# Retiming the ticks and the order inside a tick of a two-layer transformer kernel on one core

## The chip, the cores and the metric

The kernel runs on one core of a Trainium2 chip, as one launch for the whole computation. The metric is the device time of that core in microseconds (us), of which lower is better. The engines are TensorE (PE: matrix products and transposes), VectorE (DVE), ScalarE (ACT), GpSimd (POOL) and SyncE (SP), whose queue issues every DMA. Each runs its own instruction list in order, and they meet through semaphores.

## What is computed

There are 16 sequences of 512 tokens with 128 channels, in float32. Each goes through two layers:

```python
xn = _layernorm(x)
x = x + _L0_attn_ref(xn, ...) + _L0_ffn_ref(xn, ...)   # 16 causal heads of 64 channels, slopes on the distance
xn = _layernorm(x)
x = x + _L1_attn_ref(xn, ...) + _L1_ffn_ref(xn, ...)   # differential attention: 16 heads of 8, rotary
# each FFN: layernorm, 128 -> 512, silu, 512 -> 128, halved, plus its own input xn
# L1_attn: o1 - lam * o2, RMS-normalised per head, then the output product
```

## The kernel before

**Ticks.** Each sequence's first layer takes 32 ticks, and its second layer runs in the ticks of the next sequence or so. Four ticks make a round: in a round one of the eight pairs of heads of the first attention passes each stage, so several pairs are under way. A constant such as `FA_AT` says at which tick of its sequence a step that occurs once is issued; a function `tick` on each engine says in which order that engine issues what falls into a tick, for the four kinds of tick, r = 0 to 3. There is no scheduler: these numbers and this written order are the whole schedule. The branches under `late(g)` serve the last sequence's end.

**First attention.** `project_q`, `project_k`, `project_v` (L1434) make a pair's inputs; `max_scores0` (L1498) makes the scores of query block q in products of 128 to 512 columns (part 0 holds the blocks 0 and 1, then parts 2 and 3). VectorE's `row_max0` (L1195) adds the slopes, takes the maximum and empties the score tile into `pq`. ScalarE's `exp0` (L947), VectorE's `invert_sums` (L1202) and GpSimd's `scale_probs` (L816) turn it into probabilities. `turn_probs` (L1515) transposes them in three groups, 0 to 2, ScalarE's `copy_turned` (L965) empties those tiles, and `pv0` (L1528) is the product with the values.

**Second attention.** It takes 46 steps, spread over 28 ticks, one or two steps in a tick (part 0 and part 1). A step below 32 makes a pair of top tiles (`second_tops`, L1601), of which VectorE's `row_max1` (L1248) takes the row maxima. A step from 14 on makes a pair of key tiles (`second_keys`, L1587), which ScalarE's `exp1` (L987) empties. `second_values` (`pv1`, L1557) is the product with the values, one for every two key steps.

**Banks.** Two accumulator banks, `pj`, serve in turn the projections, `pv0`, the FFNs, the output products and the 128-wide transposes: a use waits until the one before the last has been read. Five banks, `sc`, serve in turn all score, top, key and turned tiles. `PJ_ORDER` and `TILES` list these uses in TensorE's order, and `bank_free` waits for the reader of the tile that had the bank:

```python
before = tile_before(i, kind, m)
...
pe.wait_ge(done, seq.upto(per, n + 1))
```

Since nearly every step makes two tiles, a step's first tile waits for the second tile of the step three before it, and its second tile waits for the first tile of the step two before it.

**Shapes on TensorE.** The tiles of `sc` are made by products and transposes over 64 of the 128 rows of the array (48 or 51 rows in use in the second attention), so that two of them run beside each other. Everything else uses all 128 rows.

**The other steps that the change names.** `ln_stats` and `ln_apply` (L1144 to L1156) are the norms on VectorE, with `ln_scale` on GpSimd between them. `ffn_act` (L913, L915) on ScalarE and `ffn_dve` (L1164) on VectorE are the FFN's activation, `add_from` (L1171) the sums out of a `pj` bank, `residual0` and `residual1` the residual on GpSimd. `rotate` (L1216 to L1228) is the rotary step with its cut into three bfloat16 parts, which `store_parts` sends to DRAM and `stack` brings back as `QS` and `KS`. `head_norm_a` and `head_norm_b` (L1256 to L1279) are the RMS norm of the heads.

## Time and profile before

| | |
|---|---|
| median of 3 runs | 2565.78 us (2561.99 to 2567.45) |
| the profiled execution | 2568.39 us |
| its span, first to last instruction | 2566.6 us |
| mean granted clock of TensorE | 0.984 |
| busy: PE, DVE, ACT, POOL | 94%, 72%, 73%, 55% |

The 32 ticks of a sequence last 153.2 us in the middle of the run. The time is that of TensorE's list and of what makes TensorE wait. In the timeline a merged row gives the time from the first start to the last end of like instructions. A wait ahead of a row is printed in brackets; a wait between two products of one row shows only in its length.

### The profile page before, as it was taken

To read this page: it belongs to the slowest core of one execution; us is meant where nothing else is said; L and a number is where in the kernel's file an instruction comes from. 1 tells how busy PE (TensorE), PEld (TensorE's weight loads), DVE (VectorE), ACT (ScalarE), POOL (GpSimd) and SP (SyncE) were. 2 spreads that over 40 slices of the span, in tenths; PEclk is the share of its full clock that TensorE was granted. 3 is DMA by queue.
4 is the path that set the end of the run, shared out by engine and by line. 5 is a ranking of instruction groups with operands and counts; after the bars stand their busy time and mean duration, and the time that the engine had idled before them with its cause. 6 is when DMAs were issued, how large, how long until landed. Compare 5 with 4: busy or idle time off the path is not lost.

```text
span 2566.6 us, 60925 instructions
## 1 busy us (share of the span) xinstructions
PE 2409.8 (94%) x22400; PEld 1162.3 (45%) x22400; DVE 1852.2 (72%) x5637; ACT 1881.1 (73%) x4707; POOL 1414.1 (55%) x1356
## 2 busy tenths in 40 slices
PE   6999999999999999999999999999999999999876
PEld 3454444444444445444444444445444444444421
DVE  4448677777877777777776877777777776867675
ACT  4866787777778777787778778777777878778445
POOL 5866474655646466474655646565464655646211
PEclk8999999999999999999999999999999999999978
DMA  3002020110202001020200202002020200202020
GB/s 93 6 6 51 6 55 2 39 22 6 55 6 51 6 18 43 6 55 2 48 13 6 55 6 54 3 18 43 6 55 2 55 6 6 55 2 55 2 55 5
DMA packets 59864, 69.11 MB, mean 27 GB/s; under 512 B 11057, under 2 KB 55345, under 8 KB 56369
## 3 DMA queue, kind: packets, MB, share of 16 engines
q1 hardware_dynamic: 59568, 65.21, 11.2%
q8 instruction: 181, 2.97, 0.5%
q14 instruction: 115, 0.93, 0.1%
HBM read 35.04 MB, written 29.36 MB: 25 GB/s over the span
## 4 chain that ended last, share of the span: by engine, by line
PE 76%; DVE 12%; ACT 6%; issue 3%; DMA 1%; POOL 0%; SPq 0%; POOLq 0%; DVEq 0%; ACTq 0%
PE pj L1434 18%; PE pj L1528 12%; PE sc L1498 11%; PE op L1557 8%; PE sc L1515 5%; PE sc L1601 5%; PE sc L1587 5%; PE pj L1454 5%; PE pj L1544 5%; DVE pq L1195 3%; DVE mx L1248 3%; PE pj L1424 2%; ACT pt L987 2%; DVE y L1216 1%; ACT pt L965 1%
## 5 line engine op out<-in xcount | busy, mean ns | idle before, releaser
L816 POOL TENSOR_SCALAR pq<-pq,rsum 128x128 f32<-128x128 f32 (+3 forms) x1024 | 1111.2, 1099 | 939.5 <-DVE rsum L1202 939.3
L1248 DVE TENSOR_REDUCE mx<-sc 128x1 f32<-128x512 f32 x1024 | 653.7, 682 | 200.7 <-PE sc L1601 199.8
L987 ACT ACTIVATE pt<-sc 128x512 f32<-128x512 f32 x1024 | 557.0, 610 | 196.0 <-PE sc L1587 192.8
L1195 DVE CUSTOM_DVE_ANT_0 pq<-sc,relkey 128x128 f32<-128x128 f32 (+3 forms) x1024 | 450.6, 486 | 213.6 <-PE sc L1498 208.8
L947 ACT ACTIVATE pq<-pq,mx 128x128 f32<-128x128 f32 (+3 forms) x1024 | 572.1, 575 | 6.9 <-DVE mx L1195 6.9
L965 ACT ACTIVATE pt<-sc 128x512 f32<-128x512 f32 (+1 forms) x768 | 356.3, 535 | 214.3 <-PE sc L1515 212.7
L1498 PE MATMUL sc<-K,Q 64*128 64x128 f32 (+3 forms) x2048 | 377.8, 466 | 18.2 <-DVE mx L1248 10.4
L1528 PE MATMUL pj<-pt,v 128*64 128x512 f32 (+3 forms) x2048 | 309.3, 444 | 10.1 <-DVE y L1216 5.8
L1434 PE MATMUL pj<-xnT,wqkv 128*64 128x512 f32 x1024 | 273.1, 622 | 12.3 <-ACT xnT L895 5.5
L1515 PEld LDWEIGHTS sc<-ident,pq 64*128 64x128 f32 x5120 | 203.0, 139 | 170.9 <-issue 131.6
L1515 PE MATMUL sc<-ident,pq 64*128 64x64 f32 x5120 | 235.4, 227 | 26.6 <-DVE mx L1195 22.5
L1557 PE MATMUL op<-pt,v 128*32 128x512 f32 x1920 | 255.7, 605 | 3.7 <-ACT pt L987 3.6
L1601 PE MATMUL sc<-KS,QS 48*128 48x512 bf16 x960 | 232.0, 381 | 22.0 <-DVE mx L1195 13.9
L1498 PEld LDWEIGHTS sc<-K,Q 64*128 64x128 f32 x2048 | 147.5, 186 | 228.5 <-issue 187.1
L1528 PEld LDWEIGHTS pj<-pt,v 128*64 128x64 f32 x2048 | 145.9, 138 | 163.8 <-issue 114.6
L947 ACT ACTIVATION_READ_ACCUMULATOR pq<-pq,mx 128x1 f32 x1024 | 218.5, 213 | 0.0
L1587 PE MATMUL sc<-QS,KS 51*128 51x512 bf16 x960 | 188.6, 384 | 2.8 <-ACT pt L987 0.9
L1434 PE MATMUL pj<-wqkv,xnT 128*64 128x128 f32 x2048 | 140.8, 280 | 5.9 <-ACT att L938 5.8
L1587 PEld LDWEIGHTS sc<-QS,KS 51*128 51x128 bf16 x960 | 47.8, 94 | 195.4 <-issue 153.7
L1601 PEld LDWEIGHTS sc<-KS,QS 48*128 48x128 bf16 x960 | 60.3, 94 | 165.3 <-DVE mx L1248 55.1
L1434 PEld LDWEIGHTS pj<-wqkv,xnT 128*64 128x64 f32 x2048 | 110.1, 137 | 50.3 <-issue 37.6
L913 ACT ACTIVATE tanh<-pj,b1h 128x512 f32<-128x512 f32 x128 | 88.2, 689 | 60.0 <-PE pj L1434 58.7
(117 smaller groups left out, 2807.1 us busy)
## 6 DMA issues: line engine op xcount, KB each, us to landing
scr_p<-y SPq DMA_DIRECT2D x160, 128.0 KB, 2.4
QS<-scr_p SPq DMA_DIRECT2D x30, 384.0 KB, 6.1
KS<-scr_p SPq DMA_DIRECT2D x30, 384.0 KB, 8.7
x_in<-in_L_attn_x SPq DMA_DIRECT2D x16, 256.0 KB, 2.8
scr_p<-tanh SPq DMA_DIRECT2D x32, 128.0 KB, 2.4
out_x<-xres SPq DMA_DIRECT2D x15, 256.0 KB, 2.3
QS<-nrow SPq DMA_DIRECT2D x180, 4.0 KB
wqkv<-in_L_attn_w_qkv SPq DMA_DIRECT2D x1, 1536.0 KB, 6.7
```

The lines of the kernel that those rows point to most:

```text
L816: pool.tensor_scalar(rows, rows, rsum[:, p % NROWS, c:c + 1], None, ALU.mult).then_inc(s_scl, 1)
L947: act.activation(rows, rows, ACT.Exp, scale=-1.0, bias=mx0[:, p % NROWS, c:c + 1], accum_out=lsum[:, p % NROWS, c:c + 1]).then_inc(s_exp0, 1)
L965: act.activation(to[:, :, h, :], sc[tile_bank(i, "tr0", m)][:, 0:cols].rearrange("p (n c) -> p n c", c=HALF), ACT.Copy).then_inc(s_ev, 1)
L987: act.activation(pt1[:, GS * (m % 2) + 2 * j + h, :], sc[tile_bank(i, "st1", 2 * n + h)][:, :], ACT.Exp, scale=float(DS) ** -0.25).then_in ...
L1195: dve.tensor_tensor_reduce(out=pq[:, at:at + width], in0=sc[tile_bank(i, "mx0", m)][:, left:left + width], in1=relkey[:, T - width:T], sca ...
L1248: dve.reduce_max(mx1[:, g % 2, at:at + 1], sc[tile_bank(i, "mx1", 2 * t + h)][:, :], AXIS.X).then_inc(s_mxd1, 1)
L1434: last = pe.matmul(t[r, c * k:c * (k + 1)], w(k)[:, r], x(k), start=True, stop=True)
L1498: last = pe.matmul(sc[tile_bank(i, "mx0", m + j)][:, left:left + width], Q0[r, b, P * row:P * (row + 1)], K0[r, b, 0:width], start=True, s ...
L1515: last = pe.transpose(sc[tile_bank(i, "tr0", m + h)][:, HALF * n:HALF * (n + 1)], pq[r, at:at + P], ident[r, r])
L1528: last = pe.matmul(t[DH * j:DH * (j + 1), P * k:T], v0[:, p % NBUF, k, DH * j:DH * (j + 1)], pt[:, base:base + WIDTH[k]], start=k == 0, st ...
L1557: last = pe.matmul(op[32 * j:32 * (j + 1), :], values1[i.last()][:, k, (GS * g + j) // 2, :], pt1[:, GS * (k % 2) + j, :], start=k == 0, s ...
L1601: pe.matmul(sc[tile_bank(i, "mx1", 2 * t + n)][:, :], queries[r, slot, P * q:P * (q + 1)], keys[r, slot, :], start=True, stop=True).then_i ...
```

## The change

It moves steps and removes or adds none. Each constant below is the tick of a step:

```diff
-X_AT = -19
-LN0_AT = (-15, -8, -1)
-XNT0_AT = -5
+X_AT = -20
+LN0_AT = (-15, -9, -2)
+XNT0_AT = -6
...
-LN1_AT = (47, 48, 54)
+LN1_AT = (46, 48, 54)
...
-STORE_AT = (49, 50)
-STACK_AT = (54, 54)
+STORE_AT = (48, 49)
+STACK_AT = (54, 55)
...
-HID0_AT = (2, 5, 7, 10)
-HID1_AT = (57, 59, 60, 61)
-ADDA_AT = 11
-ADDB_AT = 64
-ADDWA_AT = 35
+HID0_AT = (1, 6, 8, 9)
+HID1_AT = (57, 57, 60, 61)
+ADDA_AT = 12
+ADDB_AT = 63
+ADDWA_AT = 36
...
-HEAD3A_AT = 87
-HEAD3B_AT = 89
+HEAD3A_AT = 88
+HEAD3B_AT = 90
...
-PLN0_AT = (-9, -7)
-PLN1_AT = (47, 48)
-RES0_AT = 0
-RES1_AT = 53
-HEAD3P_AT = 87
-STOREOUT_AT = 91
+PLN0_AT = (-13, -8)
+PLN1_AT = (47, 49)
+RES0_AT = 1
+RES1_AT = 50
+HEAD3P_AT = 89
+STOREOUT_AT = 88
```

Inside a tick, TensorE's order is written anew for all four kinds of tick (with the bank lists `pj_order` and `score_order` to match). The third part of the scores, `max_scores0(i, p, 3)`, goes from the end of tick 2 to the head of tick 3. The top tiles go ahead of the key tiles of the same part, except for part 0 of tick 0, and a 128-row product or a group of others mostly stands between them. Here are tick 1, the head of tick 2, and tick 3 (behind its `else`):

```diff
+                elif r == 1:
+                    second_turns(h, k, 0)
+                    second_tops(h, k, 0)
+                    p, i = pair(g, 3)
+                    if i is not None:
+                        pv0(i, p)
+                    second_keys(h, k, 0)
+                    second_tops(h, k, 1)
+                    second_values(h, k, 0)
+                    second_turns(h, k, 1)
+                    second_keys(h, k, 1)
+                    others(g, h, k)
+                    second_values(h, k, 1)
+                    p, i = pair(g, 0)
+                    if i is not None:
+                        max_scores0(i, p, 2)
+                elif r == 2:
+                    second_tops(h, k, 0)
                     second_turns(h, k, 0)
                     p, i = pair(g, -1)
...
+                        project_v(i, p)
+                    second_keys(h, k, 0)
+                    others(g, h, k)
+                    second_tops(h, k, 1)
+                    second_keys(h, k, 1)
                     second_values(h, k, 0)
...
-                    second_turns(h, k, 1)
-                    p, i = pair(g, 0)
-                    if i is not None:
-                        max_scores0(i, p, 3)
                     second_values(h, k, 1)
                 else:
                     second_turns(h, k, 0)
+                    p, i = pair(g, 0)
+                    if i is not None:
+                        max_scores0(i, p, 3)
+                    second_values(h, k, 0)
+                    second_tops(h, k, 0)
+                    others(g, h, k)
                     second_turns(h, k, 1)
                     second_keys(h, k, 0)
-                    second_tops(h, k, 0)
-                    second_values(h, k, 0)
-                    others(g, h, k)
                     p, i = pair(g, 1)
                     if i is not None:
                         turn_probs(i, p, 0)
+                    second_tops(h, k, 1)
                     second_values(h, k, 1)
                     second_keys(h, k, 1)
```

ScalarE and VectorE:

```diff
+                    p, i = pair(g, -1)
+                    if i is not None:
+                        copy_q(i, p)
                     p, i = pair(g, 1)
                     if i is not None:
                         exp0(i, p, 3)
-                    p, i = pair(g, -1)
-                    if i is not None:
-                        copy_q(i, p)
                     p, i = pair(g, 2)
                     if i is not None:
                         copy_turned(i, p, 2)
+                    others(g, h, k)
                     p, i = pair(g, 2)
                     if i is not None:
...
-                    others(g, h, k)
                     p, i = pair(g, 3)
                     if i is not None:
                         copy_attention(i, p)
                     second_attention(h, k, 1)
+                    others(g, h, k)
+                    p, i = pair(g, 0)
+                    if i is not None:
+                        exp0(i, p, 1)
                 elif r == 2:
                     second_attention(h, k, 0)
+                    p, i = pair(g, -1)
+                    if i is not None:
+                        values(i, p)
+                    second_attention(h, k, 1)
                     p, i = pair(g, 0)
                     if i is not None:
-                        exp0(i, p, 1)
-                    second_attention(h, k, 1)
-                    p, i = pair(g, -1)
-                    if i is not None:
-                        values(i, p)
+                        exp0(i, p, 2)
                     others(g, h, k)
                 else:
-                    p, i = pair(g, 0)
-                    if i is not None:
...
-                    p, i = pair(g, 1)
-                    if i is not None:
-                        invert_sums(i, p, 1)
                     others(g, h, k)
-                    p, i = pair(g, 1)
-                    if i is not None:
-                        invert_sums(i, p, 2)
+                    norms(g)
                     second_attention(h, k, 0)
-                    norms(g)
                     p, i = pair(g, -1)
...
+                    if i is not None:
+                        invert_sums(i, p, 3)
                 elif r == 1:
-                    p, i = pair(g, 1)
-                    if i is not None:
-                        invert_sums(i, p, 3)
-                    norms(g)
                     second_attention(h, k, 0)
                     second_attention(h, k, 1)
                     others(g, h, k)
+                    norms(g)
                 elif r == 2:
+                    norms(g)
                     p, i = pair(g, 0)
                     if i is not None:
+                        invert_sums(i, p, 0)
+                    others(g, h, k)
+                    p, i = pair(g, 0)
+                    if i is not None:
                         row_max0(i, p, 2)
-                    norms(g)
-                    others(g, h, k)
                     second_attention(h, k, 0)
...
                     second_attention(h, k, 1)
+                    p, i = pair(g, 0)
+                    if i is not None:
+                        invert_sums(i, p, 2)
 
             pipeline(tick)
```

GpSimd scales parts 0 and 1 of a pair in tick 3 of the pair's own round, part 2 in tick 0 and part 3 in tick 2 of the next; before, part 0 was in tick 2 of its own round, part 1 in tick 0, and parts 2 and 3 in tick 2 of the next. SyncE's list is row for row the same in both kernels, since the stores and loads that got other ticks keep their order among each other.

**Place 1, TensorE, ticks 2 and 3 of a middle round.** In these rows L1498 128x512 is part 3 of the scores, L1587 a pair of key tiles, L1601 a pair of top tiles, L1515 group 0 of the turned tiles, L1434 with `hT` a piece of the FFN, and L1557 the second attention's values. Before, from part 3 on:

```order
L1498 MATMUL sc<-K,Q 128x512 x2
L1557 MATMUL op<-pt,v 32x512 x4
L1587 MATMUL sc<-QS,KS 128x512 x2
L1601 MATMUL sc<-KS,QS 128x512 x2
L1434 MATMUL pj<-hT,w 64x512 x2
L1515 MATMUL sc<-ident,pq 128x64 x16
L1557 MATMUL op<-pt,v 32x512 x4
L1587 MATMUL sc<-QS,KS 128x512 x2
L1601 MATMUL sc<-KS,QS 128x512 x2
```

Now, from part 3 on:

```order
L1498 MATMUL sc<-K,Q 128x512 x2
L1601 MATMUL sc<-KS,QS 128x512 x2
L1434 MATMUL pj<-hT,w 64x512 x2
L1587 MATMUL sc<-QS,KS 128x512 x2
L1515 MATMUL sc<-ident,pq 128x64 x16
L1601 MATMUL sc<-KS,QS 128x512 x2
L1557 MATMUL op<-pt,v 32x512 x4
L1587 MATMUL sc<-QS,KS 128x512 x2
```

The pair of key tiles that stood right behind the scores, ahead of the top tiles, now stands behind the piece of the FFN and right ahead of the turned tiles; the second top pair has moved ahead of the values.

**Place 2, TensorE, the end of tick 1 and tick 2.** L1498 128x384 is part 2 of the scores, L1434 with `wqkv,xnT` 64x128 is `project_v`. Before:

```order
L1557 MATMUL op<-pt,v 32x512 x4
L1498 MATMUL sc<-K,Q 128x384 x2
L1587 MATMUL sc<-QS,KS 128x512 x2
L1601 MATMUL sc<-KS,QS 128x512 x2
L1434 MATMUL pj<-wqkv,xnT 64x128 x8
L1587 MATMUL sc<-QS,KS 128x512 x2
L1601 MATMUL sc<-KS,QS 128x512 x2
L1434 MATMUL pj<-hT,w 64x512 x2
L1498 MATMUL sc<-K,Q 128x512 x2
```

Now:

```order
L1557 MATMUL op<-pt,v 32x512 x4
L1498 MATMUL sc<-K,Q 128x384 x2
L1601 MATMUL sc<-KS,QS 128x512 x2
L1434 MATMUL pj<-wqkv,xnT 64x128 x8
L1587 MATMUL sc<-QS,KS 128x512 x2
L1434 MATMUL pj<-hT,w 64x512 x2
L1601 MATMUL sc<-KS,QS 128x512 x2
L1587 MATMUL sc<-QS,KS 128x512 x2
L1557 MATMUL op<-pt,v 32x512 x4
L1498 MATMUL sc<-K,Q 128x512 x2
L1601 MATMUL sc<-KS,QS 128x512 x2
```

The value projection now stands between the top pair and the key pair that follow part 2, where both pairs stood in one piece behind it, and part 3 is no longer in tick 2.

**Place 3, ScalarE, ticks 2 and 3 of the same round.** L987 is `exp1` on a key pair, L932 the copy of the values, L947 `exp0`, L913 and L915 an FFN piece, L965 `copy_turned`. Before:

```order
L987 ACTIVATE pt<-sc 128x512 x2
L932 ACTIVATE v<-pj 128x512
L913 ACTIVATE tanh<-pj,b1h 128x512
L915 ACTIVATE y<-pj,b 128x512
L947 ACTIVATE pq,lsum<-pq,mx 128x384 x2
L987 ACTIVATE pt<-sc 128x512 x2
L913 ACTIVATE tanh<-pj,b1h 128x512
L915 ACTIVATE y<-pj,b 128x512
L965 ACTIVATE pt<-sc 128x8x64 x2
L987 ACTIVATE pt<-sc 128x512 x2
```

Now:

```order
L987 ACTIVATE pt<-sc 128x512 x2
L932 ACTIVATE v<-pj 128x512
L987 ACTIVATE pt<-sc 128x512 x2
L947 ACTIVATE pq,lsum<-pq,mx 128x384 x2
L913 ACTIVATE tanh<-pj,b1h 128x512
L915 ACTIVATE y<-pj,b 128x512
L987 ACTIVATE pt<-sc 128x512 x2
L913 ACTIVATE tanh<-pj,b1h 128x512
L915 ACTIVATE y<-pj,b 128x512
L965 ACTIVATE pt<-sc 128x8x64 x2
L987 ACTIVATE pt<-sc 128x512 x2
```

`exp0` of part 1 has left tick 2 for tick 1, and that of part 2 has moved from the head of tick 3 to ahead of tick 2's FFN piece. In tick 3 `exp1`, the FFN piece and `copy_turned` keep their order, but the key pair that `exp1` empties now comes later.

## Rows read from the trace of the kernel before

**Rows 1.** The head of the page: span, busy time and share of each engine.

```profile
span 2566.6 us, 60925 instructions
...
PE 2409.8 (94%) x22400; PEld 1162.3 (45%) x22400; DVE 1852.2 (72%) x5637; ACT 1881.1 (73%) x4707; POOL 1414.1 (55%) x1356
```

**Rows 2.** Windows of 32 ticks, first, middle, last: busy us and count, clock.

```profile
80.54:233.77 153.23, 140.51 (x1368) 75.69 (x1365) 86.20 (x328) 111.34 (x302) 109.45 (x106) 0.97 0.11 24
...
999.89:1153.12 153.23, 148.00 (x1406) 71.83 (x1402) 115.05 (x352) 117.12 (x294) 87.70 (x84) 1.00 0.11 26
...
2378.91:2532.14 153.23, 127.11 (x898) 48.00 (x898) 110.88 (x237) 71.90 (x147) 27.70 (x27) 0.86 0.11 24
```

**Rows 3.** TensorE timeline: start, duration, instruction, idle before it and its releaser.

```profile
1017.25 0.73 PE L1601 MATMUL sc<-KS,QS 48*128 48x512 bf16 x2
1018.29 1.09 PE L1434 MATMUL pj<-wqkv,xnT 128*64 128x128 f32 x16 [0.32 <-ACT att L938]
...
1021.36 0.38 PE L1601 MATMUL sc<-KS,QS 48*128 48x512 bf16 x1
1022.10 0.39 PE L1601 MATMUL sc<-KS,QS 48*128 48x512 bf16 x1 [0.36 <-DVE mx L1195]
```

**Rows 4.** The same timeline, later second tiles behind a score tile.

```profile
1039.08 0.38 PE L1601 MATMUL sc<-KS,QS 48*128 48x512 bf16 x1
1039.68 0.39 PE L1601 MATMUL sc<-KS,QS 48*128 48x512 bf16 x1 [0.23 <-DVE mx L1195]
...
1060.09 0.65 PE L1601 MATMUL sc<-KS,QS 48*128 48x512 bf16 x2
...
1064.61 0.39 PE L1601 MATMUL sc<-KS,QS 48*128 48x512 bf16 x1 [0.36 <-DVE mx L1195]
```

**Rows 5.** The same timeline, score products of part 2, and two top pairs.

```profile
1058.81 0.92 PE L1498 MATMUL sc<-K,Q 64*128 64x384 f32 x4 [0.56 <-ACT pt L987]
...
1151.02 0.92 PE L1498 MATMUL sc<-K,Q 64*128 64x384 f32 x4 [0.66 <-DVE mx L1248]
1151.74 0.77 PE L1601 MATMUL sc<-KS,QS 48*128 48x512 bf16 x2
...
1153.47 0.71 PE L1601 MATMUL sc<-KS,QS 48*128 48x512 bf16 x2
```

**Rows 6.** The same timeline, products that wait for a projection bank.

```profile
1008.95 1.08 PE L1434 MATMUL pj<-xnT,wqkv 128*64 128x512 f32 x4 [0.18 <-DVE xres L1171]
...
1116.34 2.37 PE L1528 MATMUL pj<-pt,v 128*64 128x512 f32 x16 [0.49 <-DVE y L1216]
...
1127.02 1.94 PE L1434 MATMUL pj<-xnT,wqkv 128*64 128x512 f32 x8 [0.40 <-ACT xnT L895]
...
1132.77 2.38 PE L1528 MATMUL pj<-pt,v 128*64 128x512 f32 x16 [0.20 <-ACT y L915]
```

**Rows 7.** The same timeline, a pair ahead of a pair, and ahead of a projection.

```profile
1028.88 0.39 PE L1587 MATMUL sc<-QS,KS 51*128 51x512 bf16 x2
1029.10 0.38 PE L1601 MATMUL sc<-KS,QS 48*128 48x512 bf16 x2
1029.41 1.08 PE L1434 MATMUL pj<-xnT,wqkv 128*64 128x512 f32 x4
```

**Rows 8.** Timeline of ScalarE: start, duration, instruction.

```profile
1045.28 1.10 ACT L987 ACTIVATE pt<-sc 128x512 f32<-128x512 f32 x2
1046.29 0.69 ACT L913 ACTIVATE tanh<-pj,b1h 128x512 f32<-128x512 f32 x1
...
1047.44 1.08 ACT L965 ACTIVATE pt<-sc 128x512 f32<-128x512 f32 x2
```

**Rows 9.** TensorE timeline again, the turned tiles of group 0 and the values.

```profile
1046.17 0.71 PE L1515 MATMUL sc<-ident,pq 64*128 64x64 f32 x16
1046.81 1.07 PE L1557 MATMUL op<-pt,v 128*32 128x512 f32 x8
```

**Rows 10.** One line of VectorE: count, ns (least, median, longest), first and last start.

```profile
L1228 DVE TENSOR_TENSOR tanh<-y x28: 691/1172/1659, 345.2 to 2346.7; 128x512 bf16<-128x512 f32 x28
```

72 lines of the change are left out of this document (28 added, 44 removed).

## The prediction

> **What bounds the kernel now.** The head of the page comes first: TensorE is busy for 2409.8 us of a span of 2566.6, with VectorE, ScalarE and GpSimd well below it [rows 1]. So the time is TensorE's list plus what holds it up. The windows say where: the middle sequences all look alike, 153.2 us for 32 ticks, 148.0 of it busy at a granted clock of 1.00, while the first window has 140.5 busy and the last 127.1 [rows 2]. Busy time hides part of the waits, because a pair of half-row products in which the second waits is printed as one longer row. I therefore went through one sequence in TensorE's timeline, from 1001 to 1154 us, and took each start that comes later than the same pair of instructions starts elsewhere. What I looked for in each row is which tile's bank was late, and whose reader was last.
>
> Unheld, the second tile of a top pair starts with the first and the row lasts 0.39 us (the form is seen in [rows 7]). Four kinds of wait stand out.
>
> (a) A top pair close behind part 2 of the scores: its second tile takes the bank that part 2's first tile had two steps before, and VectorE has not emptied it. The row at 1017.25 lasts 0.73 [rows 3], so 0.34 is wait; 0.60 passes between 1039.08 and 1039.68, and the row at 1060.09 lasts 0.65, so 0.26 [rows 4]; the row at 1151.74 lasts 0.77, so 0.38 [rows 5]. Sum 1.58 us.
>
> (b) The same behind part 3: 1021.36 to 1022.10, 0.74 [rows 3]; as much again ahead of 1064.61, which has the same printed idle of 0.36 [rows 4]; and the row at 1153.47, 0.71, so 0.32 [rows 5]. Sum 1.80.
>
> (c) Part 2 itself, behind two step pairs in one piece: 0.56 and 0.66 [rows 5]. Sum 1.22.
>
> (d) A product that needs a `pj` bank: behind the attention copy 0.32 [rows 3], behind a sum 0.18, behind the rotary product 0.49, behind the copy of the transposed norm 0.40, behind an FFN piece 0.20 [rows 6]. Sum 1.59.
>
> Together 6.2 us of a sequence's 153.2. The rest of the list is products back to back.
>
> **The change, part by part.** No step is added or removed, so the terms are waits that go, waits that come, and crossings between shapes.
>
> *Waits (a).* In the new tick 2 only the top pair follows part 2 directly, and its second tile waits for a key or top tile of the step before part 2, long read. The next pair is the key pair, and `project_v` stands in between; a projection's row is 1.08 us long [rows 7], more than any of the four waits. Where there is no key pair (1017 us), the next tile is part 3, also behind `project_v`. I take all 1.58 as gone; at worst the late `row_max0` costs the same again.
>
> *Waits (b).* Part 3 now heads tick 3, and between the top pair behind it and the next tiles stand the others of that tick (an FFN piece, an output product or a transpose in nearly every round). I take the 1.80 as gone.
>
> *Waits (c).* In tick 1 `pv0` now stands between the two step pairs, 2.3 us of a row of 2.37 [rows 6]. The tiles that part 2 waits for are then read. 1.22 gone.
>
> *Waits (d).* ScalarE's attention copy goes ahead of tick 1's FFN piece, `exp0` of part 2 leaves the head of tick 3, where it stood ahead of the transposed norms' copy; `copy_q` goes ahead of `exp0` of part 3; the second FFN's sum and the key rotation's product get ahead of their consumer. I take 1.59 gone, of which 0.2 to 0.5 (the rotary one) hangs on VectorE being free.
>
> *Crossings.* A pair costs 0.22 us from its start to the next when the next is a half-row pair (1028.88 to 1029.10) and 0.31 when it is a projection over all rows (1029.10 to 1029.41) [rows 7], so each crossing from half to all rows costs 0.09. Counted over a middle sequence in both orders there are 64 such crossings before and 61 after: 0.27 less. The Trainium skill, TensorEngine Tiling (Array Packing), Key Properties, says that changing the tiling mode drains TensorE, whichever way it changes. By that rule all changes of array shape would count, 134 before and 129 after, and at the same 0.09 the saving would be 0.45 us. The rows show it in one direction only, and I keep 0.27.
>
> *Waits that come.* In tick 3 the key pair now stands directly ahead of group 0 of the turned tiles, both read by ScalarE, and the last key pair of the tick takes the bank of the first turned tile. In the round with FFN pieces in both ticks 2 and 3, ScalarE has to do `exp1` (1.01 us to the next start), the FFN piece (1.15) and the first of two copies (0.5) before that bank is free [rows 8], 2.7 us, and by then it is still 0.4 behind with tick 2's piece and `exp0` (an estimate from the same rows). TensorE needs 2.2 us from the key pair to there: 0.22 for the pair, 0.64 for the turned tiles, 0.31 for a top pair [rows 7] and 1.0 for the values [rows 9]. The difference is a wait of some 0.9 us, where there is none now; I take 0.85. Four smaller ones of 0.2 to 0.4: in tick 2 behind the output product, where `ln_stats` now stands ahead of `row_max0`; the heads' transpose, whose copy now stands behind `exp0` of part 1; a key projection behind the last heads' norm; and the first top pair behind turned group 2 in the round where the sequence changes. They are estimates by the waits of the same kinds in [rows 5, 6], taken at 0.3: 1.2. The sum of what comes is 2.05, with 0 and 5 as bounds. The wait of 1027 us stays.
>
> *No cost taken.* SyncE's list is unchanged, so no DMA moves past another. GpSimd gets its parts earlier and more evenly; all its results are needed a round later. VectorE's inversions are small and stand later in a tick than their sums. The moved sums, norms and residuals have their readers ticks away; if that cover failed, each would cost about one operation, 0.7 us as in the pieces of [rows 8].
>
> **The sum.** Gone 6.19 + 0.27 = 6.46; come 2.05; net 4.4 us a sequence. In my laying out, about eight places pass within 0.2 us of a bank that is still being read; I take 0.1 each, 0.8 in all, off it. That leaves 3.6 us. Fourteen windows are like the middle one, and the fuller start and the thinner end count as half of one [rows 2], so 14.5 x 3.6 = 52 us. The profiled execution took 2568.4 us, 2.6 more than the median of the runs; 2568.4 - 52 = 2516, and 2.6 less on the scale of the median: 2514.
>
> **The rivals.**
>
> *Gain mostly given back to ScalarE (2548).* Key pair and turned group stand together in five of the eight rounds. If all five wait 0.6 or so rather than one 0.85, 2.4 us more come, 1.2 net remain, 17 us. For it: ScalarE is the fullest engine behind TensorE [rows 1]. Against: before, the same copies waited on nothing.
>
> *VectorE slowed by GpSimd (2537).* The last operation of a rotation takes 0.69 us at least and 1.66 at most, with a median of 1.17 [rows 10]: in the timeline the long ones are those during GpSimd's work on big tiles. GpSimd's scaling has been moved to other ticks. If now both rotations of a sequence are hit instead of one, in three operations each, VectorE loses up to 1.6 us at a place where the projections wait for it: 3.6 becomes 2.0, 29 us gained. The Trainium skill, Advanced Engine Details and Errata, GPSIMD Details, says that GpSimd shares a read and a write interface with VectorE and conflicts with its instructions of two SBUF inputs; the trace agrees for this line.
>
> *Nothing (2566).* The waits only move on to the next bank, because the readers need the same time in total. Against: VectorE and ScalarE are idle for over a quarter of the time [rows 1].
>
> *Slower (2606).* The queue on ScalarE in tick 3 grows into a steady wait: in each of the five rounds TensorE stands for `exp1` and more, 1.6 us on average, 8.0 a sequence against 6.46 less the 1.2: 2.7 us lost, 14.5 times, 40 us. It decides from 1.05 us a round on. For it: `exp1` plus an FFN piece is 2.2 us [rows 8], and `exp0`'s two new places at the ends of ticks 1 and 2 stand ahead of it. Against: in three of the five rounds tick 3 has no FFN piece.
>
> **How the numbers follow.** The forecast, 2490 to 2538 by its own bounds (waits that come between 0.8 and 4), has 0.62. ScalarE taking most back 0.13, VectorE slowed 0.06, nothing 0.06, slower 0.13. A run of this kernel tells 0.2%, some 5 us, from no change. So faster is 0.62 + 0.13 + 0.06 = 0.81, same 0.06, slower 0.13. A range from 2482 (nothing comes, 14.5 x 5.9) to 2564 leaves out the slower case and a little at either end.
>
> **What would show it.** In the profile after, a middle window of 32 ticks lasts about 149.6 us. In TensorE's timeline the top pair behind part 2 lasts 0.4, and the steps of tick 3 start evenly behind part 3; the product of part 2 has no idle ahead of it; the one new wait is a key product's second tile on ScalarE's L965. The forecast is wrong if that wait is found in every round, if L1195 comes up ahead of L1587 in tick 2, or if L1228 is at 1.6 us in both of its instances.

## The result, and the profile after

The changed kernel takes 2530.47 us (median of 4 runs, 2529.27 to 2533.2), the kernel before 2566.61 us (4 runs, 2561.99 to 2569.62) beside it. The ratio is 0.9857, 95% interval 0.9846 to 0.9869: 36 us less. The forecast was 2514, 52 us less. The direction and the range held, and the gain is two thirds of what was forecast. It also comes from other places than forecast.

The head of the page after, span and the busy time of each engine, answers to [rows 1]:

```profile
span 2531.4 us, 60926 instructions
PE 2404.7 (95%) x22400; PEld 1164.7 (46%) x22400; DVE 1850.6 (73%) x5637; ACT 1886.1 (75%) x4707; POOL 1417.6 (56%) x1356
```

TensorE's busy time has fallen by 5.1 us only, the span by 35.2. The windows of 32 ticks after, two of the middle ones (columns: busy time of each engine with its instructions, granted clock, DMA share, GB/s), answer to [rows 2]:

```profile
814.40:966.10 151.70, 147.85 (x1403) 72.02 (x1402) 115.13 (x352) 117.56 (x295) 87.80 (x84) 1.00 0.12 26
966.10:1117.80 151.70, 147.85 (x1404) 72.04 (x1402) 115.11 (x352) 117.57 (x295) 87.82 (x84) 1.00 0.12 26
```

A middle window is 151.7 us long, where 149.6 was forecast and 153.2 is that of before. To see where the 35 us are, I cut both traces at the start of each sequence's first query projection:

| stretch | before | after | difference |
|---|---|---|---|
| first sequence | 95.04 | 83.54 | -11.5 |
| second | 114.08 | 109.97 | -4.1 |
| 13 middle ones, sum | 1992.7 | 1972.6 | -20.1 |
| from the last one on, to TensorE's last product | 347.5 | 348.1 | +0.6 |

So a middle sequence gives 1.5 us and not 3.6, and the start, which the forecast counted as a part of half a window, gives 15.6.

**The start.** Three rows of TensorE's timeline of the kernel before, the last engine named being what was waited for:

```profile
58.48 5.38 PE L1454 MATMUL pj<-w,y 128*64 128x128 f32 x64 [3.34 <-DVE y L1164]
100.01 0.46 PE L1515 MATMUL sc<-ident,pq 64*128 64x64 f32 x8 [2.71 <-DVE mx L1195]
100.41 4.04 PE L1528 MATMUL pj<-pt,v 128*64 128x512 f32 x16
```

The same FFN product in the timeline of the kernel after:

```profile
51.47 1.13 PE L1498 MATMUL sc<-K,Q 64*128 64x512 f32 x4
52.52 3.71 PE L1454 MATMUL pj<-w,y 128*64 128x128 f32 x64
```

Before, TensorE waited 3.34 us for the last `ffn_dve`, which stood at tick 10 of VectorE's list behind the second layer's weights being unpacked, work of the first sequence alone. The product that followed took 5.38 us instead of 3.71. The granted clock from 58.40 to 64.00 us was 0.70; from 52.2 to 56.8 after it was 1.00. Behind the wait of 2.71 us the values product took 4.04 us where its like takes 2.37 [rows 6]. A wait in the start is paid more than once, since the clock falls behind it: granted were 1.00 in the wait itself (55.0 to 58.5 us), then 0.50 from 59.5 to 62.8, and 0.50 again from 100.5 to 103.7 behind the second one. With the 1.67 us that each product took longer, that is 5.0 us at the first place and 4.4 at the second. Another 1.6 us of the difference is no merit of the change: the two projections from 21.7 us took 3.57 us before and 1.94 after, by the clock alone, and that varies between executions (it is 3.68 in e9 below, whose list up to there is that of the kernel after). These three make 11.0 of the 11.5 us. Of the 4.1 us of the second sequence, 1.5 are what each middle one gains. The rest isn't divided here, and part of it can be the clock too: the granted clock in this stretch was 0.97 before, 0.98 after, and 1.00 in e6 and e8 below, where the stretch lasts 108.2 and 106.9 us.

**A middle sequence.** Of each TensorE instruction I took the time from the start of the one ahead of it, and called what exceeds the shortest such time of the same two kinds anywhere in the run a wait. Waits of 0.1 us and more, by who released them, in us of one middle sequence (from 1000.95 us before, from 966.1 after):

| released by | before | after |
|---|---|---|
| `row_max0` | 2.91 | 0.45 |
| `row_max1` | 1.54 | 1.55 |
| attention copy, copies of transposed norms, `rotate` | 1.58 | 0.20 |
| `exp1` | 0.71 | 2.97 |
| turned copies (L965) | 1.35 | 2.06 |
| values copy | 0 | 0.43 |
| FFN piece, sum | 0.53 | 0.57 |
| none near | 0.71 | 0.81 |
| sum | 9.3 | 9.0 |
| the products without their waits | 134.6 | 133.7 |

The waits on `row_max0` and on the copies of the `pj` banks went as the change was made to do it, 3.8 us in all; on `row_max1` as much came as went. Waits on ScalarE's `exp1` and copies of 3.4 us came in their place. The gain of 1.5 us is what this leaves of the waits, 0.3 us, then 0.9 in the products' own list and 0.3 in waits under 0.1 us.

The top pair behind part 2 of the scores, which was to last 0.4 us, does so in one of the four rounds that had a wait there before. These are the four rows of TensorE's timeline after:

```profile
974.66 0.69 PE L1601 MATMUL sc<-KS,QS 48*128 48x512 bf16 x2
...
993.19 0.52 PE L1601 MATMUL sc<-KS,QS 48*128 48x512 bf16 x2
...
1013.97 0.39 PE L1601 MATMUL sc<-KS,QS 48*128 48x512 bf16 x2
...
1034.42 0.59 PE L1601 MATMUL sc<-KS,QS 48*128 48x512 bf16 x2
```

So 0.3, 0.13, 0 and 0.2 us of wait remain there, 0.63 where it was 1.58.

TensorE's timeline of a middle sequence after, at tick 3 of the round that [rows 8] and [rows 9] show and at ticks 1 and 2 near the end of the second attention:

```profile
1020.46 0.39 PE L1587 MATMUL sc<-QS,KS 51*128 51x512 bf16 x2
1021.39 0.71 PE L1515 MATMUL sc<-ident,pq 64*128 64x64 f32 x16 [0.54 <-DVE mx L1248]
1021.91 0.41 PE L1601 MATMUL sc<-KS,QS 48*128 48x512 bf16 x2
1022.25 1.07 PE L1557 MATMUL op<-pt,v 128*32 128x512 f32 x8
1023.25 0.80 PE L1587 MATMUL sc<-QS,KS 51*128 51x512 bf16 x2
...
1075.39 1.07 PE L1557 MATMUL op<-pt,v 128*32 128x512 f32 x8 [0.37 <-ACT pt L987]
...
1079.82 1.06 PE L1557 MATMUL op<-pt,v 128*32 128x512 f32 x8 [0.37 <-ACT pt L987]
```

The last key pair of tick 3 at 1023.25 lasts 0.80 instead of 0.39: its second tile waits 0.41 for the copy of turned group 0, the wait that was forecast (at 0.85). Three lines above, at 1021.39, the first turned tile waits for a row maximum, 0.71 us in all, which was not forecast. And the two values products wait for `exp1`, 0.44 each in all: they start 0.64 us after the last transpose, where the kernel's last sequence has 0.20 (e8's expectation has 0.53 for it; 0.37 is printed idle). No step of the forecast had looked at them. In the groups by line this is TensorE's L1557, whose idle time rose from 3.7 us to this:

```profile
L1557 PE MATMUL op<-pt,v 128*32 128x512 f32 x1920 | 256.7, 607 | 19.7 <-ACT pt L987 18.2
```

**The crossings.** Two value projections of 16 products in TensorE's timeline after, each with the row that follows:

```profile
993.64 1.09 PE L1434 MATMUL pj<-wqkv,xnT 128*64 128x128 f32 x16
994.56 1.03 PE L1434 MATMUL pj<-hT,w 128*64 128x512 f32 x4
...
1014.28 1.09 PE L1434 MATMUL pj<-wqkv,xnT 128*64 128x128 f32 x16
1015.31 0.39 PE L1587 MATMUL sc<-QS,KS 51*128 51x512 bf16 x2
```

From start to start it is 0.92 us when all rows go on and 1.03 when a half-row pair follows. So the crossing costs 0.1 us from all rows to half rows too, beside the 0.09 of the other way [rows 7]. Between 240 and 2200 us of the trace after, the last product of such a projection takes 0.10 us to the start of an FFN or rotary product over all rows (38 times, never more than 0.103) and 0.205 to that of a half-row pair (52 times). There are 64 crossings each way before and 61 after, six fewer, 0.6 us. The Trainium skill, TensorEngine Tiling (Array Packing), Key Properties, says that a change of tiling mode drains TensorE, and names no direction in which it would not; this trace agrees. The prediction had the rule and kept to one direction.

### The profile page after: what moved, and what is told of

Read it like the earlier page. It is cut to its first block, busy times and chain, and to the rows that moved or that the text cites. A ratio compares the mean times of both kernels' runs of the same rounds, so it can differ in the third digit from the quotient of the medians.

```text
span 2531.4 us, 60926 instructions
## 1 busy us (share of the span) xinstructions
PE 2404.7 (95%) x22400; PEld 1164.7 (46%) x22400; DVE 1850.6 (73%) x5637; ACT 1886.1 (75%) x4707; POOL 1417.6 (56%) x1356
## 3 DMA queue, kind: packets, MB, share of 16 engines
q8 instruction: 181, 2.97, 0.5%
## 4 chain that ended last, share of the span: by engine, by line
PE 81%; DVE 9%; ACT 6%; issue 2%; DMA 1%; SPq 0%; POOL 0%; POOLq 0%; ACTq 0%; DVEq 0%
PE pj L1434 20%; PE pj L1528 12%; PE sc L1498 11%; PE op L1557 9%; PE sc L1587 6%; PE sc L1515 5%; PE sc L1601 5%; PE pj L1544 5%; PE pj L1454 5%; ACT pt L987 4%; DVE mx L1248 3%; DVE pq L1195 3%; PE pj L1424 2%; ACT v L932 1%; DVE K L1178 0%
## 5 line engine op out<-in xcount | busy, mean ns | idle before, releaser
L816 POOL TENSOR_SCALAR pq<-pq,rsum 128x128 f32<-128x128 f32 (+3 forms) x1024 | 1126.6, 1113 | 822.6 <-DVE rsum L1202 820.4
L1248 DVE TENSOR_REDUCE mx<-sc 128x1 f32<-128x512 f32 x1024 | 653.2, 681 | 211.0 <-PE sc L1601 211.0
L987 ACT ACTIVATE pt<-sc 128x512 f32<-128x512 f32 x1024 | 556.3, 606 | 337.0 <-PE sc L1587 334.2
L947 ACT ACTIVATE pq<-pq,mx 128x128 f32<-128x128 f32 (+3 forms) x1024 | 574.4, 579 | 15.6 <-DVE mx L1195 15.5
L965 ACT ACTIVATE pt<-sc 128x512 f32<-128x512 f32 (+1 forms) x768 | 357.5, 543 | 77.6 <-PE sc L1515 75.7
L1498 PE MATMUL sc<-K,Q 64*128 64x128 f32 (+3 forms) x2048 | 374.5, 463 | 2.2 <-ACT pt L965 0.3
L1434 PE MATMUL pj<-xnT,wqkv 128*64 128x512 f32 x1024 | 271.6, 618 | 6.8 <-DVE xres L1171 2.9
L1557 PE MATMUL op<-pt,v 128*32 128x512 f32 x1920 | 256.7, 607 | 19.7 <-ACT pt L987 18.2
L1515 PEld LDWEIGHTS sc<-ident,pq 64*128 64x128 f32 x5120 | 208.1, 139 | 145.4 <-issue 121.6
L1515 PE MATMUL sc<-ident,pq 64*128 64x64 f32 x5120 | 232.7, 226 | 30.6 <-DVE mx L1195 20.9
L1498 PEld LDWEIGHTS sc<-K,Q 64*128 64x128 f32 x2048 | 149.3, 186 | 219.1 <-issue 156.9
L1601 PE MATMUL sc<-KS,QS 48*128 48x512 bf16 x960 | 219.6, 386 | 5.3 <-DVE mx L1248 2.3
L947 ACT ACTIVATION_READ_ACCUMULATOR pq<-pq,mx 128x1 f32 x1024 | 222.4, 217 | 0.0
L1587 PE MATMUL sc<-QS,KS 51*128 51x512 bf16 x960 | 204.8, 387 | 5.7 <-ACT pt L987 0.5
L1587 PEld LDWEIGHTS sc<-QS,KS 51*128 51x128 bf16 x960 | 50.8, 93 | 215.3 <-issue 162.2
L1434 PE MATMUL pj<-wqkv,xnT 128*64 128x128 f32 x2048 | 141.8, 281 | 0.0
L1434 PEld LDWEIGHTS pj<-wqkv,xnT 128*64 128x64 f32 x2048 | 110.7, 138 | 50.0 <-issue 47.5
L1601 PEld LDWEIGHTS sc<-KS,QS 48*128 48x128 bf16 x960 | 61.2, 95 | 139.0 <-DVE mx L1248 51.7
L913 ACT ACTIVATE tanh<-pj,b1h 128x512 f32<-128x512 f32 x128 | 87.7, 685 | 48.8 <-PE pj L1434 48.8
```

The costliest lines, as they stand in the source:

```text
L816: pool.tensor_scalar(rows, rows, rsum[:, p % NROWS, c:c + 1], None, ALU.mult).then_inc(s_scl, 1)
L947: act.activation(rows, rows, ACT.Exp, scale=-1.0, bias=mx0[:, p % NROWS, c:c + 1], accum_out=lsum[:, p % NROWS, c:c + 1]).then_inc(s_exp0, 1)
L987: act.activation(pt1[:, GS * (m % 2) + 2 * j + h, :], sc[tile_bank(i, "st1", 2 * n + h)][:, :], ACT.Exp, scale=float(DS) ** -0.25).then_in ...
L1248: dve.reduce_max(mx1[:, g % 2, at:at + 1], sc[tile_bank(i, "mx1", 2 * t + h)][:, :], AXIS.X).then_inc(s_mxd1, 1)
L1434: last = pe.matmul(t[r, c * k:c * (k + 1)], w(k)[:, r], x(k), start=True, stop=True)
L1498: last = pe.matmul(sc[tile_bank(i, "mx0", m + j)][:, left:left + width], Q0[r, b, P * row:P * (row + 1)], K0[r, b, 0:width], start=True, s ...
```

## The experiments

First, second and middle sequence are the stretches of the table above, each from the one execution that was profiled; the middle one is the median of 13. The ratio is to the kernel before timed beside the run. Its median lay between 2565.5 and 2571.2 us from one set of runs to the next, so ratios compare more closely than times. The kernel after has 0.9857 (0.9846 to 0.9869).

| run | us | ratio to before (95%) | first | second | middle |
|---|---|---|---|---|---|
| e1_hid0_only | 2574.3 | 1.0014 (1.0004 to 1.0023) | 91.0 | 115.1 | 153.8 |
| e2_hid0_norm0 | 2582.9 | 1.0048 (1.0035 to 1.0061) | 86.3 | 116.0 | 154.7 |
| e3_ticks_only | 2573.1 | 1.0013 (1.0004 to 1.0021) | 86.7 | 114.0 | 154.2 |
| e4_orders_only | 2603.4 | 1.0124 (1.0111 to 1.0137) | 89.3 | 112.3 | 156.1 |
| e5_orders_norm0 | 2572.6 | 1.0016 (1.0003 to 1.0028) | 89.3 | 110.0 | 154.0 |
| e6_residual_late | 2553.1 | 0.9940 (0.9925 to 0.9954) | 83.5 | 108.2 | 153.3 |
| e7_hidden_later | 2534.4 | 0.9869 (0.9854 to 0.9883) | 83.3 | 109.9 | 151.9 |
| e8_values_late | 2527.1 | 0.9843 (0.9826 to 0.9859) | 83.4 | 106.9 | 151.5 |
| e9_v_behind_keys | 2530.8 | 0.9858 (0.9841 to 0.9874) | 86.9 | 110.0 | 151.7 |
| e10_pv_ahead | 2545.9 | 0.9918 (0.9903 to 0.9933) | 83.6 | 110.1 | 152.9 |
| e11_keys_first | 2537.7 | 0.9887 (0.9872 to 0.9901) | 83.7 | 110.5 | 152.1 |
| e12_copies_half | 2523.9 | 0.9829 (0.9806 to 0.9853) | 85.4 | 110.5 | 151.1 |

**e1 and e2: the start's ticks alone.** The kernel before with `HID0_AT = (1, 6, 8, 9)`, and in e2 the first norm's ticks too:

```diff
-HID0_AT = (2, 5, 7, 10)
+HID0_AT = (1, 6, 8, 9)
-LN0_AT = (-15, -8, -1)
+LN0_AT = (-15, -9, -2)
-PLN0_AT = (-9, -7)
+PLN0_AT = (-13, -8)
```

(e1 has the first pair of lines only; e2 also `X_AT` and `XNT0_AT`, one tick earlier.)

> The kernel before, with HID0_AT = (1, 6, 8, 9) alone. Theory 1: in the first sequence VectorE's last FFN piece stood behind the preparation of the second layer's weights, which made TensorE wait 3.34 us, and the clock that fell in this wait made the output product 5.38 us long instead of 3.71. Then the stretch from the first q projection of sequence 0 to that of sequence 1 (95.0 us) gets shorter by about 5.0 us, and the 32 ticks of a middle sequence stay within 0.5 us of 153.2: 2566 - 5 = 2561. Rival: the shorter start comes from the order inside the ticks; then this changes nothing.

> The kernel before, with HID0_AT and the first norm's four constants (X_AT, LN0_AT, XNT0_AT, PLN0_AT) of the changed one. Theory 1: the wait of 2.71 us ahead of the turned tiles at 100 us, behind the norms of the next sequence on VectorE, and the 1.67 us by which the following values product was longer, go as well: the first 95.0 us shrink by about 9.4, the time to 2557, plus or minus what a middle sequence gives (within 0.5 us each, so 7). Rival: the norms' wait stays, since in the order of before VectorE does them ahead of the scores in that tick anyway; then 2561 as with the FFN pieces alone.

The first sequence falls by 4.0 us and then by 4.7, in all 8.7 where 9.4 was expected. e1 loses the wait of 3.34 us and e2 both waits. The 64 FFN products take 3.71 us in both runs, the values product 2.38 in e2, and 3.55 in e1, which keeps the wait of 2.71 ahead of it. So both terms of the start are what the theory has. The times missed: 2561 and 2557 were expected, and both runs are slower than the kernel before, since the middle sequence rises by 0.6 and 1.5 us and not by under 0.5. The same ticks cost in the old orders.

**e3 and e4: the two halves of the change.** e3 has all the new ticks with the orders of before, e4 all the new orders with the ticks of before.

> All the constants of the changed kernel, the written orders of before. Theory 1 (the middle sequences gain by the order inside the ticks, the start by the constants): a middle sequence stays within 0.5 us of 153.2, the start is 10 to 15 us shorter, time 2551 to 2558. Rival (constants and orders each bring part of both): a middle sequence at about 152.4 and the time at about 2548.

> The written orders of the changed kernel, all constants of before. Theory 1: a middle sequence at 151.7 to 152.3, the start little shorter, time 2541 to 2551. Rival (the orders suit only their own constants): a middle sequence at 153 or more and a time not under 2566.

Neither half makes the kernel faster. For e3 neither the theory nor its rival holds, for e4 the rival does. A middle sequence costs 1.0 us more with the ticks alone and 2.9 more with the orders alone, and 1.5 less with both: 5.4 us a sequence come from the two together. TensorE's timeline of e4 has two waits that neither kernel has in this size:

```profile
811.55 1.08 PE L1434 MATMUL pj<-xnT,w_l 128*64 128x512 f32 x4 [1.22 <-DVE K L1178]
857.67 0.66 PE L1424 MATMUL pj<-ident,hn 128*128 128x128 f32 x4 [2.18 <-DVE hn L1156]
```

**e5: the orders with the first norm's ticks**, the four constants of e2 without `HID0_AT`.

> The written orders of the changed kernel with the first norm's four constants of it (X_AT, LN0_AT, XNT0_AT, PLN0_AT), all other constants of before. Theory 2: the constants have to fit the orders. In the orders alone the transpose of the next sequence's second norm waits 2.25 us for VectorE (L1156), since the new order puts the norm of tick -1 where nothing covers it, and about 1 us more of the products right behind it; with the norm a tick earlier this goes: a middle sequence falls from 156.1 to about 153, the time from 2603 to about 2558. Rival (the loss of the orders alone is spread over many places): not more than 1 us a sequence comes back, 2585 or more.

The wait for `hn` is gone (a middle sequence 154.0 instead of 156.1, where 153 was expected), the wait for the last `copy_k` stays in the same size. On VectorE `ln_apply` heads its tick in both orders. But the new orders have TensorE make the top pair ahead of it behind the 64 products of the FFN: in e4 VectorE takes that pair's maxima from 854.36 us and begins the norm at 855.56, for 2.05 us where it took 1.10 in the kernel before, and TensorE has nothing left to do from 855.5 on. One tick earlier the norm is out of the way; the new orders are affordable only with their ticks.

**e6: the residual back at its tick.** The kernel after with one constant changed:

```diff
-RES1_AT = 50
+RES1_AT = 53
```

> The changed kernel with RES1_AT back at 53. Theory 2: GpSimd's residual over two big tiles then runs beside VectorE's rotation, L1228 or L1224 takes 1.65 us instead of 0.69 in one of the two rotations, the copy of the keys behind it comes late and the second rotary product waits for its bank: 1.0 to 1.4 us more a sequence, 15 to 21 us in all, about 2547. Rival (VectorE has time to spare there): the rotation is 1 us longer and a sequence stays at 151.7.

A middle sequence costs 1.64 us more, as the theory has it (1.0 to 1.4 expected), and the second rotary product waits 1.23 us for `copy_k`, as in e4 and e5. If the two add, the norm's ticks (2.1 us) and this one (1.64) make 3.7 of the 4.4 us that lie between e4's middle sequence and that of the kernel after. VectorE's timeline of e6 ahead of it, then GpSimd's:

```profile
940.75 0.69 DVE L1224 TENSOR_TENSOR y<-y 128x512 f32<-128x512 f32 x1
941.48 1.39 DVE L1226 CAST y<-y 128x512 bf16<-128x512 f32 x1
942.90 1.65 DVE L1228 TENSOR_TENSOR tanh<-y 128x512 bf16<-128x512 f32 x1
944.48 0.68 DVE L1178 COPY K<-pj 128x512 f32<-128x512 f32 x1
```

```profile
941.07 1.51 POOL L801 TENSOR_TENSOR xacc<-xacc,xn 128x512 f32<-128x512 f32 x1
942.66 1.34 POOL L805 TENSOR_TENSOR xacc<-xacc,bias 128x512 f32<-128x512 f32 x1
```

The rotation's last two operations take 1.39 and 1.65 us while GpSimd adds the residual, and `copy_k` behind them is late by that. Each of the two ends only after GpSimd's addition beside it has ended (942.58 and 944.00 us), by 0.29 and 0.55 us. In the kernel after the residual is three ticks earlier, and the rotation's last operation takes 691 ns at least, 693 in the middle and 694 at most, where [rows 10] has 691, 1172 and 1659:

```profile
L1228 DVE TENSOR_TENSOR tanh<-y x32: 691/693/694, 178.4 to 2425.3; 128x512 bf16<-128x512 f32 x32
```

The Trainium skill, Advanced Engine Details and Errata, GPSIMD Details, tells of this conflict; here it is worth 14 times 1.64, 23 us, more than the middle sequences gain. The prediction had the mechanism as a rival in the wrong direction: it feared that the change would add such meetings, and the change takes them away. The kernel before had the meeting too (its operation at 1111.26 us took 1.65), but in its orders a values product stands ahead of the second rotary product, and no wait of 0.1 us or more names `copy_k` in its middle sequence: what waited behind the rotation there was 0.49 [rows 6]. The 1.64 us is what the meeting costs in the new orders.

**e7 and e8: two of the waits that remain.** In e7 VectorE has `row_max0` of part 2 ahead of the others in tick 2; in e8 TensorE has the values product of part 1 in tick 1 behind part 2 of the scores:

```diff
-                    second_values(h, k, 1)
                     p, i = pair(g, 0)
                     if i is not None:
                         max_scores0(i, p, 2)
+                    second_values(h, k, 1)
```

> The changed kernel with VectorE's row_max0 of part 2 ahead of the others in tick 2, instead of behind them. If the wait of 0.71 us ahead of the turned tiles in the round of the second FFN piece comes from that piece standing ahead of row_max0 (0.6 us) on VectorE, it falls to about 0.1, and a sequence to about 151.2; the time falls by up to 8 us, to about 2525. Rival (the wait is for VectorE's three row maxima in sequence, however they start): no change in that wait, 2530 to 2535, since the FFN pieces come later.

> The changed kernel with the values product of part 1 behind part 2 of the scores in tick 1. Theory: the wait of 0.53 us ahead of the values in tick 1 (for exp1 of the key pair just issued) goes, since the scores' 0.9 us stand in between; a sequence falls to about 151.2 and the time by some 7 us. Rival: the score product's bank is not free yet there, and the wait goes over to it: 151.7 as before, 2530.

e7 leaves the 0.71 us at the first turned tile as it was and costs 0.15 us a middle sequence: what is late there isn't the order of tick 2. e8 takes the wait at tick 1 away and gains only 0.2 us a middle sequence, since the transpose in tick 2 now waits for ScalarE's copy into `oraw` (0.23 printed). Its second sequence is 3.1 us shorter, but at a granted clock of 1.00 instead of 0.98, so that is not shown to be its merit. At 2527.1 it is 3.4 us below the kernel after, where the two intervals overlap.

**e9: the value projection behind the key pair.** This undoes in tick 2 what the prediction had the waits (a) go by:

```diff
+                    second_keys(h, k, 0)
                     p, i = pair(g, -1)
                     if i is not None:
                         project_v(i, p)
-                    second_keys(h, k, 0)
```

> The changed kernel, with the value projection of tick 2 of a round behind the key pair, as before the change, and not between the top pair and the key pair. My theory (the prediction's waits (a) were removed by the projection that stands behind the top pair): the key pair's second tile takes a bank that was read late, so waits of 0.3 to 0.6 us come back at that pair in each of the four rounds that have this tick's part 2 or 3 ahead, 1.5 to 2 us a sequence, a middle sequence of 153.3 us and a ratio to the changed kernel of about 1.010, so 2552 us. Rival (the waits of tick 2 went with the smoother supply of score parts, not with the projection's place): no wait comes back, within 4 us of 2530.

The middle sequence is 151.7 us, as after, and the time is 2530.8: my theory falls. One wait came, at one of the four places. TensorE's timeline of e9, the second tile of the key pair:

```profile
866.17 0.38 PE L1587 MATMUL sc<-QS,KS 51*128 51x512 bf16 x1
866.78 0.39 PE L1587 MATMUL sc<-QS,KS 51*128 51x512 bf16 x1 [0.23 <-DVE mx L1195]
```

It is 0.60 us. In exchange three waits behind it are shorter: ahead of part 3 in tick 3 of the next round (0.20 became 0.11), at a values product behind part 3 (0.27 became under 0.10) and at another (0.44 became 0.29). So at three of the four places (a) went with something else in the new lists. Which of it, the place of the top pair or VectorE's order, no run here separates.

**e10: `pv0` ahead of the pairs**, which undoes what the waits (c) were to go by:

```diff
+                    p, i = pair(g, 3)
+                    if i is not None:
+                        pv0(i, p)
                     second_tops(h, k, 0)
-                    p, i = pair(g, 3)
-                    if i is not None:
-                        pv0(i, p)
```

> The changed kernel, with the first layer's values product (pv0) of tick 1 ahead of the top pair, as before the change, so that two top and key pairs follow each other without it. My theory (the prediction's waits (c) were removed by pv0 between the pairs): waits of 0.5 to 0.6 us come back in tick 1 wherever there is a pv0, two or more to a sequence, so 1 to 1.5 us a sequence, a middle sequence of 152.9 and about 2548 us. Rival (banks are free by then in either order): no wait comes back, within 4 us of 2530.

The middle sequence costs 1.18 us more, where (c) was 1.22. Part 2 of the scores waits 0.66 us for `row_max1` again, as in the second row of (c) in [rows 5]. In place of the first, which was for `exp1`, a top pair's second tile waits for `row_max1`; TensorE's timeline of e10:

```profile
886.28 0.38 PE L1601 MATMUL sc<-KS,QS 48*128 48x512 bf16 x1
887.00 0.39 PE L1601 MATMUL sc<-KS,QS 48*128 48x512 bf16 x1 [0.35 <-DVE mx L1248]
```

**e11: the key pair of tick 3 earlier**, ahead of the FFN piece, output product or transpose:

```diff
                     second_tops(h, k, 0)
+                    second_keys(h, k, 0)
                     others(g, h, k)
                     second_turns(h, k, 1)
-                    second_keys(h, k, 0)
```

> The changed kernel, with the key pair of part 0 in tick 3 ahead of the tick's other products (FFN piece, output product or transpose) and not behind them and turned group 1. My theory (the waits of tick 3, 0.4 to 0.5 us in each of five rounds, stand behind ScalarE, which gets exp1 and two turned copies in one piece): exp1 can begin earlier, the waits of the last key pair behind the turned copy fall by half, 1 us a sequence less, a middle sequence of 150.7 and about 2516 us. Rival (ScalarE's whole list of the tick is what is late, so an earlier begin only moves the wait to the pair itself, which takes a bank of part 3's time): the waits stay in sum, 2530 plus or minus 6, or slower.

The rival is right: 0.44 us more a middle sequence. TensorE's timeline of e11:

```profile
848.45 0.37 PE L1587 MATMUL sc<-QS,KS 51*128 51x512 bf16 x1
849.03 0.39 PE L1587 MATMUL sc<-QS,KS 51*128 51x512 bf16 x1 [0.21 <-DVE mx L1195]
849.34 3.71 PE L1544 MATMUL pj<-wout,att 128*64 128x128 f32 x64
...
853.76 0.38 PE L1587 MATMUL sc<-QS,KS 51*128 51x512 bf16 x1
854.48 0.39 PE L1587 MATMUL sc<-QS,KS 51*128 51x512 bf16 x1 [0.35 <-ACT pt L965]
```

The pair now waits for `row_max0` of part 3 (0.58 at the second tile, and 0.73 in two other rounds), and the tile behind the turned copy waits 0.72 where it was 0.49. In exchange the waits on `exp1` in this tick and the 0.71 at the first turned tile are gone. By kind, in a middle sequence: on `row_max0` 2.0 us more, on `exp1` 1.2 less, on `row_max1` 0.4 less. The waits changed their names and grew a little.

**e12: less work for ScalarE**, all instructions in their places:

```diff
-                act.activation(to[:, :, h, :], sc[...][:, 0:cols]...
+                w = cols if i.first() or i.last() else cols // 2
+                act.activation(to[:, 0:w // HALF, h, :], sc[...][:, 0:w]...
```

> The changed kernel, in which ScalarE's copies of the turned probabilities (48 of a sequence) take only the first half of their columns in all sequences but the first and the last; the rest of the destination keeps what an earlier sequence left, so the attention output is not the reference's. Every instruction stays in its place, and ScalarE has 0.2 us less in each copy, by the two forms of its row (0.61 and 0.41 us), 9.6 us a sequence. Waits of TensorE that name ScalarE's exp1 or its turned copies add up to 5.2 us of a middle sequence of the changed kernel. My theory (the step that failed is the waits that come, and they are ScalarE being late): the waits at and behind the turned groups shrink by up to 0.4 us each and go by 2 us or more in sum, a middle sequence under 149.8 and at most 2504 us. Rival (ScalarE is only the last of several readers that are late, VectorE's row maxima are next): the waits change their name to row_max and the middle sequence falls by under 0.7, 2520 us or more.

The copies are 0.2 us shorter, ScalarE has 7.2 us less in a window (110.3 instead of 117.6; 9.6 was expected), and a middle sequence falls by 0.57 us, as small a gain as the rival had. Two rows of e12's timeline (its line numbers are one higher), the waits that were 0.49 and 0.44 after:

```profile
1001.94 0.66 PE L1588 MATMUL sc<-QS,KS 51*128 51x512 bf16 x2
...
1074.81 1.06 PE L1558 MATMUL op<-pt,v 128*32 128x512 f32 x8 [0.37 <-ACT pt L988]
```

The waits that name a turned copy fell from 2.05 to 1.33 us in sum (the first row lasts 0.66, so 0.27 is wait). The row maxima took 0.4 of it back: at two top pairs 0.13 and 0.22 became 0.33 and 0.43. The waits on `exp1` are as they were, to 0.1 us in sum. ScalarE's timeline of the kernel after shows why, at three of them:

```profile
1000.93 1.09 ACT L987 ACTIVATE pt<-sc 128x512 f32<-128x512 f32 x2 [3.15 <-PE sc L1587]
...
1043.04 1.08 ACT L987 ACTIVATE pt<-sc 128x512 f32<-128x512 f32 x2 [3.62 <-PE sc L1587]
...
1074.25 1.08 ACT L987 ACTIVATE pt<-sc 128x512 f32<-128x512 f32 x2 [0.40 <-PE sc L1587]
```

ScalarE had been idle for 3.15, 3.62 and 0.40 us when the key pair let `exp1` go. At these places it isn't late; its two operations take 1.08 us together, and TensorE comes to the tile that they read, or to the values that they make, sooner than that. At the turned copies its own work does count, as the 0.7 us there show: in the round of 1021 us it goes from `exp1` at 1020.88 over the FFN piece to the copy at 1022.99 without a pause, and e12 halves the wait behind that copy (0.41 to 0.20).

## Why the prediction was right or wrong

**The bound** was right: TensorE's list plus its waits, 94% busy before and 95% after.

**Waits (a) and (b), 3.4 us.** Of (b) under 0.15 us is left. Of (a) 0.63 is, at the top pairs themselves (the rows of 974 to 1034 us above), where the forecast took nothing. Its reading was wrong at two of the four places: the trace of before names `row_max1` (L1248) as what released the second tiles at 1017.59 and 1152.13, so the tile read late was a top tile there and not part 2. The reason given for (a), the projection that stands in between, fell in e9 at three places of four. And at 1021.39 a new wait of 0.71 us on `row_max1` stands where the forecast had none.

**Waits (c), 1.22 us**: right in size (e10: 1.18) and in that `pv0` between the pairs removes them; one of e10's two waits is at another tile than before the change.

**Waits (d), 1.59 us**: those on the attention copy, the norm's copy and the rotary product went, 1.4 us; those behind the sum and the FFN piece stayed (0.29 and 0.28).

**Crossings, 0.27 us**: mis-sized. Both directions cost 0.1 us, so six crossings fewer give 0.6, and the list as a whole became 0.9 us shorter.

**Waits that come, 2.05 us**: this is the step of the sum that failed, though the time lies in the stated range. "In the round with FFN pieces in both ticks 2 and 3" was one wait of 0.85 and "four smaller ones" 1.2; the trace shows 3.4 us more of waits on ScalarE, and 0.71 on a row maximum. At the place of the forecast 0.85 the queue that it added up is there: from the key pair at 1020.46 us to the free bank at 1023.67 it is 3.2 us, where the forecast had 3.1. But TensorE itself was held for 0.71 us ahead of the turned tiles, which the forecast did not have, so 0.41 was left. The others are in tick 3 and behind it in the other rounds, and at the values products, which the forecast did not follow although their new places were in the order. There no queue makes them: ScalarE was idle ahead of `exp1` (e12), and what lasts is the way from the key pair over `exp1` to the next use. The rival "ScalarE takes most back", at 0.13, came nearer: waits in four of the five rounds where it had all five, 2.6 us in all where it had 3.0, and its 1.2 us a sequence is nearer to the measured 1.5 than the forecast's 3.6. By itself it would have given 2548; the start made the rest.

**The start, "half a window"**: 1.8 us forecast, 15.6 measured, of which at least 1.6 is the clock of that execution. The waits of 3.34 and 2.71 us were in the trace of before and weren't looked at, since I had read the middle closely and the ends in windows only. Two errors, 30 us too much in the middle and 14 too little at the start, partly cancelled, which is luck.

**VectorE slowed by GpSimd**: the sign was wrong. The meeting was there before, at little cost to TensorE, and is gone after; left in place it would have cost 1.64 us a sequence (e6). Without the residual's new tick the whole change is worth 14 us instead of 36.

## What to carry to other kernels

Where orders and due times are changed together, forecast them together: here each half alone was slower (by 0.13% and 1.24%) and the pair 36 us faster. Read the first and the last stretch row by row, as closely as a middle one, because a long wait there was followed by products at a lower clock. And for each product that is moved, follow its own inputs and not only the banks: the time from a product over its reader back to the next product that needs it is a fixed length, which taking other work off that engine doesn't shorten (in e12 ScalarE had 7.2 us less to do, and the waits on `exp1` stayed).

## What the runs showed of the hardware

A wait of TensorE costs more than its length at the start: after 3.34 us of waiting, 64 products took 5.38 us instead of 3.71, at a granted clock of 0.70. It isn't bound to the start, and it doesn't come each time. In e4 TensorE waits 2.2 us for `hn` in every sequence. Behind one such wait the next projection took 1.96 us (702.78 us), behind another 1.08 (859.19). The four of its 13 middle sequences that have a granted clock of 1.00 throughout last 155.0 to 155.3 us, the nine with a low stretch 156.0 to 156.8. Such low stretches vary between executions of nearly the same list (0.72 in e9 and 0.99 in the kernel after from 13.7 to 30 us), so single sequences at the start compare to within some 3.4 us only (83.5 and 86.9), while the medians of e9 and the kernel after differ by 0.4. Beside GpSimd's additions of two tiles, VectorE's cast of 0.43 us took 1.39 and its two-input operation of 0.69 us took 1.65 (e6); beside GpSimd's scaling, two-input operations of the same rotation took 0.95 to 0.97. And a crossing between all rows and half rows costs 0.1 us in either direction.
